# Layer 0's expert stage: a third bank for the up products, and gate, product, down product, result copy and store one to two steps later

## The chip, the cores and the metric

The kernel runs on one core of a Trainium2 chip. The metric is the device time of one execution in microseconds (us). It is given as the median of several runs; the profile comes from one further execution of the same program. The core's engines work side by side, each through its own list of instructions in order, and wait for each other by semaphores: TensorE (PE in the profile, its loads of weights PEld), VectorE (DVE), ScalarE (ACT), GpSimd (POOL) and SyncE (SP), which only issues transfers.

## The reference, cut to what matters

The program computes two layers. Each is a cross attention of 32 sequences of 128 tokens, width 128, over 77 context rows, and then a mixture of 8 experts of which every token uses 2. The change is in layer 0's experts:

```python
scores = x @ Wr.T + br                                  # 4096 tokens, 8 experts
idx    = top_k(scores + biases_N, 2)                    # two experts per token
val    = softmax(scores) at idx, divided by their sum
h      = x @ Wl1[n] + bl1[n]                            # 128 -> 512, a and b halves of 256
y      = (silu(a) * b) @ Wl2[n] + bl2[n]                # 256 -> 128
out    = sum over the token's two experts of val * y
x      = x + tanh(g_ffn[0]) * out
```

Layer 1 has attention with 16 heads and experts with one up product of 256, gelu and no biases.

## The kernel before, in words

**Blocks.** Tokens are sorted by expert. Each token's normalized row is scattered twice (once for each of its experts) into a list `x_rows` in device memory, and this list is worked through in blocks of 128 rows that share an expert: 71 blocks (0 to 70) in layer 0, 63 in layer 1. The block's result goes to `y_list`, also in device memory. Later GpSimd gathers for each of the 32 tiles of 128 tokens the two results of every token (`load`, two indirect transfers, line 1979), and VectorE adds them to the residual `x_res` (`combine`, line 1819).

**The plan.** `order()` (line 364) writes one list of tasks for the whole program. Every engine walks through the same list and issues its own part of each task, so the list fixes the order on every engine. `expert_steps` (line 302) yields the expert stage step by step. Before the change, step s of layer 0 had these tasks in this order:

1. `up` of block s-2. TensorE: four products of 128x128 into one bank of PSUM (line 1185), `UP_BANK[i % 2]`, two banks in turn. ScalarE, in the same task: the `gate`, silu of the first two quarters with bias, two instructions (line 1396).
2. `fetch` of a block some ten steps ahead. SyncE: one transfer from `x_rows` (line 869).
3. `turn` of block s. TensorE transposes the rows (line 1174); ScalarE copies them to `xb` (line 1379) and copies half of the expert's weights to a ring of four (line 1386); VectorE copies the other half (line 1783), after it has read the expert's number from a table.
4. `hide` of block s-2. VectorE: (third and fourth quarter + bias) * gate, two instructions (line 1791), written to `hidden`.
5. `down` of block s-4. TensorE: two products (line 1205) into `Y_BANK[i % 2]`. VectorE, in the same task: result plus bias to `y_sb` (line 1807).
6. `store` of block s-5. ScalarE's queue: one transfer of `y_sb` to `y_list` (line 1405).

Behind these a step can have late tasks: routing of the last tokens (steps 5 to 13: the tasks mturn, route, pick, rank and totals), the tables of the second part (blocks, steps 16 to 20, and block_bias at 22), at every second step from 30 to 44 one of eight `places` tasks (five VectorE instructions, lines 1750 to 1758), the loads and combines of tiles 0 to 11 (steps 53 to 73), and preparation of layer 1's attention (`clear`, `k1`, `k_load`, `norm`, `normalize`, `xt`, `q1`, `q_load`).

**Waits that matter here.** The up product of block i waits for `hidden` of block i-2, since both use one bank (line 1182). The down product of block i waits for the result copy of block i-2, for the same reason (line 1192). The gate of block i waits for `hidden` of block i-2 (the gate has two buffers). `hidden` has three buffers, `block_w` and `xb` four, `y_sb` six. The load of tile b waits for the stores of all blocks that can hold its tokens: for tiles 0 to 11 blocks 0 to 46. A tile's `gathered` buffer is one of three.

**Around the stage.** The first steps of the expert stage lie between the last steps of attention 0 (one each), and its last steps between the first of attention 1. Before the change steps 0 to 3 followed attention's steps 32 to 35; attention's step 35 has, among others, the normalization of the last group of tokens (line 1310, four ScalarE instructions, which wait until an earlier scatter has left the buffer) and a tanh (line 1373). At the other end 73 steps stood alone, and the first step of attention 1 (`score1`, line 1007, and VectorE's `row_max`, line 1445) followed step 73.

**Banks of PSUM.** There are eight. In the expert stage 0 and 1 are UP_BANK, 2 and 3 X_BANK (turns), 4 and 6 Y_BANK; SPLIT_BANK (5) and ROUTE_BANK (7) are used by the late tasks.

Of the kernel before, what the change touches and what calls it, by code (L numbers as in the profile page):

```python
# [66 lines left out]
UP_BANK = (0, 1)  # L67
X_BANK = (3, 2)
# [233 lines left out]
def expert_steps(layer, tasks, begun, after):  # L302
# [13 lines left out]
    for b in range(AMONG[layer]):  # L316
        begins = FIRST_DONE[layer] + 6 + (8 * b // 5 if layer == 0 else 11 * b // 10)
        loads.setdefault(begins, []).append(("load", layer, b))
        combines.setdefault(begins + 3, []).append(("combine", layer, b))
# [3 lines left out]
    for s in range(max(max(combines) + 1, n_blocks + 4 + (layer == 0))):  # L323
        step = []
        if 0 <= s - 2 < n_blocks:
            step.append(("up", first + s - 2))
        for _ in range(2):
# [6 lines left out]
        if layer == 0 and 0 <= s - 2 < n_blocks:  # L334
            step.append(("hide", s - 2))
        if 0 <= s - 4 < n_blocks:
            step.append(("down", first + s - 4))
        if 0 <= s - 4 - (layer == 0) < n_blocks:
            step.append(("store", first + s - 4 - (layer == 0)))
# [24 lines left out]
def order():  # L364
# [9 lines left out]
    phases = [(attention0_steps(tasks[0]), NSEQ), (expert_steps(0, tasks[0], NSEQ + 4, after0), BLOCKS[0] + 2),  # L374
# [21 lines left out]
def flamingo_two_layers(nc, a, out):  # L396
# [79 lines left out]
    with ExitStack() as stack:  # L476
# [261 lines left out]

        def hiddens(n):
# [184 lines left out]
        def _(pe):  # L924
# [7 lines left out]
            def split_task(t):  # L932
# [41 lines left out]
                else:  # L974
                    c0 = t[1] * GK
                    w.wait_ge("weights1", 6)
                    done = three_pass(banks[:, bank, 0:GK], w1_h[:, 1, :], w1_l[:, 1, :],
# [82 lines left out]
            for t in plan:  # L1060
# [114 lines left out]
                elif kind == "up":  # L1175
# [6 lines left out]
                    w.wait_ge("hidden", hiddens(i - 1))  # L1182
                    w.wait_ge("xb", i + 1)
                    for part in range(4 if layer == 0 else 2):
                        done = pe.matmul(banks[:, UP_BANK[i % 2], part * P:(part + 1) * P], block_w[:, i % WR, part // 2, part % 2 * P:(part % 2 + 1) * P], xb[:, i % BR, :],  # L1185
# [57 lines left out]
        def _(act):  # L1243
# [12 lines left out]
            for t in plan:  # L1256
# [131 lines left out]
                elif kind == "up":  # L1388
                    i = t[1]
                    layer, k, n = of_block(i)  # L1390
                    w.wait_ge("up", i + 1)
                    if layer == 0:
                        w.wait_ge("hidden", hiddens(i - 1))
                        w.wait_ge("block_bias", k + 1)
                        for half in (0, 1):
                            act.activation(gate[:, i % 2, half, :], banks[:, UP_BANK[i % 2], half * P:(half + 1) * P], ACT.Silu,  # L1396
                                           bias=block_bias[:, k, half, n:n + 1]).then_inc(sem("gate"))
                    else:
# [616 lines left out]
```

## Time and profile before

| | |
|---|---|
| runs | 740.4, 739.4, 742.06 us |
| median | 740.4 us |
| the profiled execution | 740.05 us |
| its span, first to last instruction | 738.3 us |
| mean granted clock of TensorE in it | 0.958 |
| busy: PE, PEld, DVE, ACT, POOL | 85%, 77%, 75%, 60%, 60% |
| layer 0's expert stage in the span | about 240 to 376 us |

How to read it: the times of the profile count from the span's start. "Busy" is the time in which an engine worked on an instruction. An idle time is put down to what ended it, the releaser; "issue" is time in which the engine waited for nothing that the profile shows. PE and PEld overlap. A line number is one of the kernel before.

### The profile page before, as it was taken

The numbers are of one execution on the slowest core, as the hardware profiler recorded it, in microseconds if no ns is written. First come the engines' busy times: TensorE is split into PE (matmuls) and PEld (weight loads), VectorE is DVE, ScalarE is ACT, GpSimd is POOL, SyncE is SP. The second block draws the span as 40 slices with busy tenths as digits, with TensorE's granted clock in tenths as the row PEclk, the third lists the DMA queues.
The fourth block names the chain that finished last, engine by engine and source line by source line (L and its number), as shares of the span: only waits on it lengthen the run. The fifth ranks groups of instructions, "written<-read, shape, count | busy, mean of one in ns | idle before, by whom it ended". The sixth has DMA issues, their size and how long they took to land.

```text
span 738.3 us, 16455 instructions
## 1 busy us (share of the span) xinstructions
PE 624.7 (85%) x4501; PEld 566.0 (77%) x4501; DVE 555.6 (75%) x1931; ACT 443.0 (60%) x1275; POOL 442.1 (60%) x658
## 2 busy tenths in 40 slices
PE   6879789888885889789877888889979898789997
PEld 5668778888775779789766777778868787579885
DVE  3368588888886588888778879868897795655784
ACT  2477567867754556567666666756766654434462
POOL 4034347778766642305658778876756668766752
PEclk9999999999997999999989999989999999999999
DMA  9445658444432345335524525424234102423455
GB/s 259 138 118 135 183 169 221 130 134 137 139 112 78 99 125 157 89 95 143 155 72 121 122 73 111 123 58 120 90 79 108 44 21 89 129 89 96 146 173 165
DMA packets 132774, 89.48 MB, mean 121 GB/s; under 512 B 31508, under 2 KB 121780, under 8 KB 132652
## 3 DMA queue, kind: packets, MB, share of 16 engines
q1 hardware_dynamic: 108540, 62.83, 32.1%
q0 software_dynamic: 7904, 17.19, 7.3%
q10 hardware_dynamic: 16240, 8.41, 4.0%
q8 instruction: 38, 0.62, 0.4%
q14 instruction: 52, 0.43, 0.2%
HBM read 50.73 MB, written 39.85 MB: 123 GB/s over the span
## 4 chain that ended last, share of the span: by engine, by line
PE 37%; DVE 27%; ACT 14%; issue 8%; POOL 7%; DMA 3%; SPq 2%; DVEq 2%; ACTq 0%; POOLq 0%
PE banks L1185 7%; PE banks L1048 5%; PE banks L1205 4%; POOL gathered L1979 3%; ACT prob L1317 2%; DVE row_max L1445 2%; PE banks L1226 2%; PE banks L928 2%; PE banks L1033 2%; PE banks L1216 2%; PE banks L1015 2%; DVE row_max L1492 1%; ACT xm L1310 1%; ACT vo L1327 1%; POOL v_flat L1932 1%
## 5 line engine op out<-in xcount | busy, mean ns | idle before, releaser
L1970 POOL DMA_INDIRECT x_rows<-xm,row x120 | 121.0, 1008 | 36.2 <-issue 27.9
L1185 PE MATMUL banks<-xb,up 128*128 128x128 f32 x820 | 119.9, 284 | 24.4 <-DVE hidden L1791 11.6
L1185 PEld LDWEIGHTS banks<-xb,up 128*128 128x128 f32 x820 | 106.3, 197 | 35.4 <-issue 13.9
L1979 POOL DMA_INDIRECT gathered<-y_list,row x64 | 62.6, 978 | 52.4 <-issue 51.1
L1048 PE MATMUL banks<-v_flat,prob_t 128*128 128x108 f32 (+2 forms) x640 | 85.6, 282 | 8.4 <-POOL v_flat L1932 6.0
L1048 PEld LDWEIGHTS banks<-v_flat,prob_t 128*128 128x128 f32 (+1 forms) x640 | 78.5, 195 | 17.1 <-issue 10.6
L1342 ACT ACTIVATE prob_t<-banks 128x512 f32<-128x512 f32 x192 | 73.4, 440 | 26.8 <-PE banks L1015 25.9
L1205 PE MATMUL banks<-down,hidden 128*128 x536 | 83.6, 280 | 1.7 <-DVE y_sb L1809 1.2
L1985 POOL DMA_INDIRECT y_rows<-y_sb,result_at x63 | 60.7, 964 | 30.5 <-issue 12.1
L1932 POOL TENSOR_TENSOR v_flat<-v_raw,row_head 104x64 f32<-104x64 f32 (+1 forms) x128 | 55.8, 464 | 32.1 <-ACT v_raw L1358 31.7
L1205 PEld LDWEIGHTS banks<-down,hidden 128*128 128x128 f32 x536 | 72.2, 196 | 2.3 <-issue 2.3
L1898 POOL TENSOR_TENSOR prob<-prob,inv_sum 128x616 f32<-128x616 f32 x32 | 39.1, 1223 | 54.7 <-DVE inv_sum L1508 54.6
L1396 ACT ACTIVATE gate<-banks,block_bias 128x128 f32<-128x128 f32 x142 | 44.2, 363 | 41.2 <-PE banks L1185 39.4
L1445 DVE TENSOR_REDUCE row_max<-banks 128x8 f32<-128x616 f32 x64 | 50.3, 786 | 9.1 <-PE banks L1007 9.1
L1015 PE MATMUL banks<-ident,prob 128*128 128x128 f32 (+1 forms) x375 | 55.8, 281 | 0.3 <-POOL prob L1898 0.3
L1783 DVE COPY up<-up 128x256 f32 x134 | 42.9, 320 | 16.4 <-issue 8.3
L1033 PE MATMUL banks<-vo_flat,prob_t 128*128 128x128 f32 (+1 forms) x320 | 48.7, 307 | 5.1 <-ACT prob_t L1342 2.9
L1033 PEld LDWEIGHTS banks<-vo_flat,prob_t 128*128 128x128 f32 (+1 forms) x320 | 45.6, 219 | 6.3 <-ACT prob_t L1342 3.9
L1791 DVE SCALAR_TENSOR_TENSOR hidden<-banks,block_bias,gate 128x128 f32<-128x128 f32 x142 | 42.8, 343 | 9.0 <-ACT gate L1396 8.0
L1317 ACT ACTIVATE prob<-banks,row_max 128x77 f32<-128x77 f32 x128 | 30.8, 324 | 29.7 <-DVE row_max L1492 29.7
L1015 PEld LDWEIGHTS banks<-ident,prob 128*128 128x128 f32 (+1 forms) x375 | 45.6, 146 | 1.5 <-POOL prob L1898 0.5
L1358 ACT ACTIVATE v_raw<-banks 128x512 f32<-128x512 f32 x64 | 28.0, 437 | 30.8 <-PE banks L1107 30.8
(251 smaller groups left out, 1660.4 us busy)
## 6 DMA issues: line engine op xcount, KB each, us to landing
vo_flat<-v_rows SPq DMA_DIRECT2D x32, 256.0 KB
x_norm<-x_rows SPq DMA_DIRECT2D x74, 72.0 KB
v_rows<-vo SPq DMA_DIRECT2D x38, 128.0 KB
y_list<-y_sb ACTq DMA_DIRECT2D x71, 64.0 KB
x_far<-x_rows SPq DMA_DIRECT2D x60, 72.0 KB
q_rows<-up_raw SPq DMA_DIRECT2D x8, 512.0 KB
q_even<-q_rows SPq DMA_DIRECT2D x12, 256.0 KB
q_odd<-q_rows SPq DMA_DIRECT2D x12, 256.0 KB
```

What stands on the lines that cost most here:

```text
L1015: done = pe.transpose(banks[0:chunk_rows[c], PT_BANK[k], c % 4 * SEQ:(c % 4 + 1) * SEQ], flat[:, c * P:c * P + chunk_rows[c]], ident[:, :])
L1033: done = pe.matmul(banks[:, O_BANK, 0:D], prob_t[0:rows, b % 2, c, :], vo_flat[0:rows, b % 2, c, :], start=c == 0, stop=c == CHUNKS - 1)
L1048: done = pe.matmul(banks[:, O_BANK, half * width:half * width + cols], prob_t[0:rows, u % 2, c, :], v1_flat[0:rows, first:first + cols], s ...
L1185: done = pe.matmul(banks[:, UP_BANK[i % 2], part * P:(part + 1) * P], block_w[:, i % WR, part // 2, part % 2 * P:(part % 2 + 1) * P], xb[: ...
L1205: done = pe.matmul(banks[:, Y_BANK[i % 2], 0:D], hidden[:, i % HR, half, :], of_expert(flat[:, (2 * layer + half) * D:], i, D), start=half ...
L1317: done = act.activation(prob[:, b % 2, h, :], banks[:, S_BANK[1], h % 4 * NKEY:(h % 4 + 1) * NKEY], ACT.Exp, bias=row_min[:, b % 2, h:h + ...
L1342: act.activation(dst, banks[0:rows, PT_BANK[k], 0:len(chunks) * SEQ], ACT.Copy).then_inc(sem("prob_t"))
L1445: dve.tensor_reduce(m_view, s_view, AX.X, ALU.max).then_inc(sem("row_max"))
L1932: pool.tensor_tensor(v1_rows[0:rows, b % 2, half, chunks[0]:chunks[-1] + 1, :, 0:DK1], v1_raw[0:rows, chunks[0]:chunks[-1] + 1, half, :, : ...
L1970: pool.indirect_dma_start(out=x_rows[layer][:, :], out_offset=bass.IndirectOffsetOnAxis(ap=row[:, n, c:c + 1], axis=0), in_=xm[:, i % 2, j ...
L1979: pool.indirect_dma_start(out=gathered[:, b % GR, n, :], out_offset=None, in_=y_list[0:blocks_of_tile(0, b) * P, :], in_offset=bass.Indire ...
L1985: pool.indirect_dma_start(out=y_rows[:, :], out_offset=bass.IndirectOffsetOnAxis(ap=result_at[:, i % (2 * YR):i % (2 * YR) + 1], axis=0), ...
```

## The change

Layer 0's up products get three banks in turn: 0, 1 and a third, which is SPLIT_BANK for blocks below 28 and ROUTE_BANK from there on. The wait for `hidden` becomes that of the block which had the bank before. Up products in SPLIT_BANK wait for the last split of attention 0, those in ROUTE_BANK for the last biases, and `k1` waits until the first 28 blocks are hidden.

In layer 0 the parts of a block are tasks of their own and come later. In step s: `up` s-2 as before, `gate` s-3 (was s-2), `turn` s as before, `hide` s-3 (was s-2), `down` s-5 (was s-4), `keep`, the result copy, s-6 (was s-4, with down), `store` s-7 (was s-5). Loads and combines of layer 0 begin two steps later, and with them the preparation of attention 1; 75 steps stand alone instead of 73. In layer 1 down, keep and store stand in one step as before.

```diff
+UP_SWITCH = 28
@@ expert_steps
-        begins = FIRST_DONE[layer] + 6 + (8 * b // 5 if layer == 0 else 11 * b // 10)
+        begins = FIRST_DONE[layer] + (8 + 8 * b // 5 if layer == 0 else 6 + 11 * b // 10)
...
-    for s in range(max(max(combines) + 1, n_blocks + 4 + (layer == 0))):
+    for s in range(max(max(combines) + 1, n_blocks + (7 if layer == 0 else 4))):
...
             step.append(("up", first + s - 2))
+        if layer == 0 and 0 <= s - 3 < n_blocks:
+            step.append(("gate", s - 3))
...
-        if layer == 0 and 0 <= s - 2 < n_blocks:
-            step.append(("hide", s - 2))
-        if 0 <= s - 4 < n_blocks:
-            step.append(("down", first + s - 4))
-        if 0 <= s - 4 - (layer == 0) < n_blocks:
-            step.append(("store", first + s - 4 - (layer == 0)))
+        if layer == 0:
+            if 0 <= s - 3 < n_blocks:
+                step.append(("hide", s - 3))
+            if 0 <= s - 5 < n_blocks:
+                step.append(("down", s - 5))
+            if 0 <= s - 6 < n_blocks:
+                step.append(("keep", s - 6))
+            if 0 <= s - 7 < n_blocks:
+                step.append(("store", s - 7))
+        elif 0 <= s - 4 < n_blocks:
+            step += [("down", first + s - 4), ("keep", first + s - 4), ("store", first + s - 4)]
@@ order
-    phases = [(attention0_steps(tasks[0]), NSEQ), (expert_steps(0, tasks[0], NSEQ + 4, after0), BLOCKS[0] + 2),
+    phases = [(attention0_steps(tasks[0]), NSEQ), (expert_steps(0, tasks[0], NSEQ + 4, after0), BLOCKS[0] + 4),
@@ new functions
+        def up_bank(i):
+            if i >= BLOCKS[0]:
+                return UP_BANK[i % 2]
+            return (UP_BANK[0], UP_BANK[1], SPLIT_BANK if i < UP_SWITCH else ROUTE_BANK)[i % 3]
+        def up_before(i):
+            first = 0 if i < BLOCKS[0] else BLOCKS[0]
+            return max([j for j in range(first, i) if up_bank(j) == up_bank(i)], default=first - 1)
@@ TensorE, k1
+                    w.wait_ge("hidden", 2 * UP_SWITCH)
@@ TensorE, up
-                    w.wait_ge("hidden", hiddens(i - 1))
+                    w.wait_ge("hidden", hiddens(up_before(i) + 1))
+                    if up_bank(i) == SPLIT_BANK:
+                        w.wait_ge("split_lo", xt_count(NG - 1))
+                    elif up_bank(i) == ROUTE_BANK:
+                        w.wait_ge("block_bias", 2)
@@ ScalarE (waits and instructions of the gate as before, in a task of their own)
-                elif kind == "up":
+                elif kind == "gate":
...
+                elif kind == "up" and t[1] >= BLOCKS[0]:
@@ VectorE
-                elif kind == "down":
+                elif kind == "keep":
```

## Rows read from the trace of the kernel before

**Rows 1.** Stretches: busy us (instructions) PE, PEld, DVE, ACT, POOL; clock, DMA share, GB/s.

```profile
296.00:330.00 34.00, 27.08 (x226) 25.67 (x225) 29.27 (x110) 18.99 (x68) 6.67 (x6) 1.00 0.35 92
...
330.00:345.00 15.00, 15.00 (x137) 15.00 (x137) 11.93 (x43) 11.54 (x43) 5.01 (x6) 1.00 0.51 136
```

**Rows 2.** Timeline of one free step: start, duration, instruction, idle before.

```profile
340.08 1.06 PE L1185 MATMUL banks<-xb,up 128*128 128x128 f32 x8
...
340.98 0.27 PE L1174 MATMUL banks<-ident,x_norm 128*128 128x128 f32 x1
...
341.08 0.61 PE L1205 MATMUL banks<-down,hidden 128*128 x4
...
341.18 0.62 ACT L1396 ACTIVATE gate<-banks,block_bias 128x128 f32<-128x128 f32 x2 [0.35 <-PE banks L1185]
...
341.53 1.06 PE L1185 MATMUL banks<-xb,up 128*128 128x128 f32 x8
...
341.69 0.28 ACT L1379 ACTIVATE xb<-banks 128x128 f32<-128x128 f32 x1
...
341.83 0.61 DVE L1791 SCALAR_TENSOR_TENSOR hidden<-banks,block_bias,gate 128x128 f32<-128x128 f32 x2
...
342.38 0.29 DVE L1807 TENSOR_TENSOR y_sb<-banks,down_bias 128x128 f32<-128x128 f32 x1
```

**Rows 3.** Groups by line, 240 to 376 us: busy, mean ns, idle before.

```profile
L1185 PE MATMUL banks<-xb,up 128*128 128x128 f32 x568 | 78.6, 283 | 17.0 <-DVE hidden L1791 11.6 <-ACT up L1386 2.2 <-DVE up L1783 2.0
...
L1205 PE MATMUL banks<-down,hidden 128*128 x284 | 44.3, 280 | 0.4 <-DVE y_sb L1807 0.4
```

**Rows 4.** Timeline, the start of the expert stage.

```profile
238.62 1.28 ACT L1396 ACT_TABLE_LOAD   x1
...
241.65 0.62 ACT L1396 ACTIVATE gate<-banks,block_bias 128x128 f32<-128x128 f32 x2 [1.74 <-PE banks L1185]
...
244.13 1.13 PE L1185 MATMUL banks<-xb,up 128*128 128x128 f32 x8 [1.41 <-DVE hidden L1791]
...
244.71 1.65 ACT L1310 ACTIVATE xm<-x_res,m_shift,m_rstd 128x128 f32<-128x128 f32 x4 [1.96 <-DMA x_rows<-xm,row]
...
246.35 0.60 ACT L1396 ACTIVATE gate<-banks,block_bias 128x128 f32<-128x128 f32 x2
...
246.99 0.61 DVE L1791 SCALAR_TENSOR_TENSOR hidden<-banks,block_bias,gate 128x128 f32<-128x128 f32 x2 [1.90 <-ACT gate L1396]
...
247.31 0.61 ACT L1396 ACTIVATE gate<-banks,block_bias 128x128 f32<-128x128 f32 x2
...
247.85 1.13 PE L1185 MATMUL banks<-xb,up 128*128 128x128 f32 x8 [2.03 <-DVE up L1783]
```

**Rows 5.** Timeline, weight copies of VectorE one places period apart.

```profile
316.64 0.29 DVE L1783 COPY up<-up 128x256 f32 x1
...
320.58 0.29 DVE L1783 COPY up<-up 128x256 f32 x1
```

**Rows 6.** Timeline of ScalarE, the table load of attention 1.

```profile
376.71 1.28 ACT L1332 ACT_TABLE_LOAD   x1
...
378.02 0.72 ACT L1332 ACTIVATE prob<-prob 128x616 f32<-128x616 f32 x1
```

**Rows 7.** The chain that ended last, at the first gathers: start, duration.

```profile
335.93 1.53 DMA y_list<-y_sb
...
338.47 1.05 POOL gathered L1979
...
347.32 4.05 DMA gathered<-y_list,row
```

**Rows 8.** Timeline: last gather, last combine, attention 1 first row_max.

```profile
371.90 0.94 POOL L1979 DMA_INDIRECT gathered<-y_list,row  x1 [0.30 <-issue]
...
375.71 0.73 DVE L1819 SCALAR_TENSOR_TENSOR x_res<-gathered,token_w,x_res 128x128 f32<-128x128 f32 x2
...
376.36 0.79 DVE L1445 TENSOR_REDUCE row_max<-banks 128x8 f32<-128x616 f32 x1
```

More of the change, by code:

```diff
@@ L1181, in _ @@
                     w.wait_ge("shifted", NSEQ + layer * U1)
-                    w.wait_ge("hidden", hiddens(i - 1))
+                    w.wait_ge("hidden", hiddens(up_before(i) + 1))
[3 more added lines that the diff above has]
+                        w.wait_ge("block_bias", 2)
                     w.wait_ge("xb", i + 1)
                     for part in range(4 if layer == 0 else 2):
-                        done = pe.matmul(banks[:, UP_BANK[i % 2], part * P:(part + 1) * P], block_w[:, i % WR, part // 2, part % 2 * P:(part % 2 + 1) * P], xb[:, i % BR, :],
+                        done = pe.matmul(banks[:, up_bank(i), part * P:(part + 1) * P], block_w[:, i % WR, part // 2, part % 2 * P:(part % 2 + 1) * P], xb[:, i % BR, :],
                                          start=True, stop=True)
@@ L1387, in _ @@
                                        ACT.Copy).then_inc(sem("block_w_act"))
-                elif kind == "up":
+                elif kind == "gate":
                     i = t[1]
-                    layer, k, n = of_block(i)
+                    _, k, n = of_block(i)
                     w.wait_ge("up", i + 1)
[L1392 to L1398, printed above, removed]
-                        w.wait_ge("y_mm", i - HR + 1)
-                        act.activation(hidden[:, i % HR, :, :].rearrange("p t n -> p (t n)"), banks[:, UP_BANK[i % 2], 0:HID1], ACT.Gelu).then_inc(sem("hidden"))
+                    w.wait_ge("hidden", hiddens(i - 1))
+                    w.wait_ge("block_bias", k + 1)
+                    for half in (0, 1):
+                        act.activation(gate[:, i % 2, half, :], banks[:, up_bank(i), half * P:(half + 1) * P], ACT.Silu,
+                                       bias=block_bias[:, k, half, n:n + 1]).then_inc(sem("gate"))
+                elif kind == "up" and t[1] >= BLOCKS[0]:
+                    i = t[1]
+                    w.wait_ge("up", i + 1)
+                    w.wait_ge("y_mm", i - HR + 1)
+                    act.activation(hidden[:, i % HR, :, :].rearrange("p t n -> p (t n)"), banks[:, up_bank(i), 0:HID1], ACT.Gelu).then_inc(sem("hidden"))
                 elif kind == "store" and t[1] < BLOCKS[0]:
@@ L1790, in _ @@
                     for half in (0, 1):
-                        dve.scalar_tensor_tensor(hidden[:, i % HR, half, :], banks[:, UP_BANK[i % 2], (2 + half) * P:(3 + half) * P],
+                        dve.scalar_tensor_tensor(hidden[:, i % HR, half, :], banks[:, up_bank(i), (2 + half) * P:(3 + half) * P],
                                                  block_bias[:, k, 2 + half, n:n + 1], gate[:, i % 2, half, :], ALU.add, ALU.mult).then_inc(sem("hidden"))
-                elif kind == "down":
+                elif kind == "keep":
                     i = t[1]
```

## The prediction

> **What bounds the kernel now.** I read clock and span first (one core, nothing disturbed), then busy time by stretches, the idle time ahead of the up products, and last the timeline of the expert stage and of what follows it. The change touches layer 0's expert stage alone, roughly 240 to 376 us of the 738.3 us span.
>
> Where the stage runs freely TensorE is full: busy 15.00 of 15.00 us [rows 1], and one step follows the other in 1.45 us (up products at 340.08 and 341.53) [rows 2]. A step is 13 passes (8 up, 1 turn, 4 down) of about 0.11 us. There the 0.35 us that ScalarE waits ahead of each gate costs nothing, and a third bank gives nothing: the next up product already starts without a wait.
>
> What can be won is TensorE's idle time ahead of the up products, 17.0 us in all, against 0.4 us ahead of the down products [rows 3]. Going through the timeline I sort the 18 waits of over 0.2 us into three kinds:
> - The start: two waits, 1.41 and 2.03 us. VectorE's hidden product waited 1.90 us for a gate, and ScalarE had stood 1.96 us before it on the scatter of x_rows [rows 4].
> - Eight waits on the two-step beat of "places" between 300 and 330 us, 6.9 us in sum. There TensorE is busy 27.08 of 34 us, VectorE 29.27 [rows 1]. VectorE has two steps' and one places' work from the weight copy at 316.64 to the one at 320.58, nearly without a gap: 3.94 us [rows 5]. TensorE needs 2.90. VectorE is the bound.
> - Eight single waits, 6.5 us in sum, each behind a long VectorE task (totals, tables, norm).
>
> **The change part by part.**
>
> *Banks and lag.* Call U the end of a step's up product (341.14). Now the gate starts right after U, hidden ends at U+1.30 and the result copy at U+1.53 [rows 2]. The up product two steps on reuses the bank and starts at U + 2 x 1.45 - 1.06 = U+1.84, so VectorE may be 0.54 us late. After the change the gate stands behind xb and weight copy of the step before. That xb can start with the end of the turn, about U+0.16 (340.98 + 0.27, and a signal). Gate, xb and copy take ScalarE 0.96 us when it catches up (246.35, 247.31 [rows 4]), 0.51 of them from gate to xb, so 0.45 from xb to the next gate: U+0.61. Gate 0.62, then hidden until U+1.9 and the copy until U+2.1. With three banks hidden has until U+3.29. But the result copy has its own date: down of block s-5 still waits for the copy of s-7, and this is now issued one step before it, where it was two. That down starts as an up product ends (341.08), so at U+2.84. The slack is 0.7 us instead of 0.54: the third bank is undone by the two banks of Y_BANK. I expect 0.18 us from each single wait, 8 x 0.18 = 1.4, and 0.18 once from the places stretch, where VectorE's work stays what it is and only its lead at the beginning counts: 1.6. Against it, VectorE reads route, rank and totals in the same step in which TensorE makes them; there it has no lead, while its date is earlier by one step (1.45, less the 0.85 us by which its step otherwise ends earlier: 0.6). I charge that once. Taken: **-1.0 us**. Ends: -6.8 (8 waits x 0.85, if all the lead came through) and +3.0 (five such steps at 0.6).
>
> *The table load at the start.* ACT_TABLE_LOAD for the gate's function stands right ahead of the first gate: 1.28 us at 238.62, and ScalarE had nothing to do until 241.65 [rows 4]. That of attention's exp likewise stands right ahead of its first exp [rows 6]. Gate 0 moves from step 2 to step 3, and between them lie attention's last tasks, the four normalizations that wait for the scatter until 244.71 among them. So the load would start at about 246.35, where gate 1 now starts, on the path that runs from the normalizations through gate and hidden (246.99) to the up product at 247.85 [rows 4]. Gate 0 takes gate 1's place, and the fourth up product still needs the xb and the weight copy behind it. The cover was ScalarE's idle time; without it nothing hides the load: **+1.28 us**. Other end: 0, if it is placed earlier.
>
> By the Trainium skill, "ScalarE: Activation LUTs", section "What ACT_TABLE_LOAD costs", a switch is the load's 1283 ns and a drain of about 1380 ns. The trace has the first figure and not the second: the next activation starts at 378.02, 0.03 us behind the load's end [rows 6]. By the page the sum below would be 1.4 us higher.
>
> *Stores and gathers.* GpSimd's gathers of layer 0's results are a chain of their own: 24 of them at 1.25 us (0.95 and 0.30 of issue), 2.5 us for a tile, while tiles come up every 8/5 steps, 2.32 us. So the steps don't pace GpSimd once it has started. It starts at 338.47, behind the store of block 46, which the chain has from 335.93; its eighth gather took 4.05 us to land [rows 7]. Its last starts at 371.90, the last combine at 375.71 (3.81 us on) and attention's first row_max right behind, at 376.36 [rows 8]. The change puts store, load and combine two steps later: +2.90. The store stands behind xb, which no longer waits for the gate pair (0.51 us [rows 2]): -0.5. That the drain's steps are short doesn't help, for it is GpSimd that is late. At the far end there is some slack: of the 34.4 us from 338.47 to 372.84 the gathers take 24 x 1.25 = 30.0, and not all of the rest (norm, waits for combines) need recur. Taken -0.5. Sum **+1.9 us**. Ends: +2.9, and +0.5 if there is slack enough to leave the drain alone.
>
> *Drain.* One down product (0.61) and one result copy (0.28) more now stand ahead of attention's first score, partly beside gate and hidden of the last block: +0.5. The gathers' +1.9 lies beside it and hides it.
>
> *The rest.* Store and copy of one y_sb slot stay five steps apart; hidden and block_w keep their distances. k1's new wait for 56 hidden halves is passed when k1 comes (step 34, block 27 hidden at step 30). ROUTE_BANK is used from block 29 on, after the biases of step 22. Fetches, queues and tails on SP are as far ahead of their turns as before. Layer 1 gets the same instructions in the same order. All 0, with these distances as cover. Attention 1 hangs on its first row_max, and GpSimd on VectorE there, so I pass the shift on whole; 0 is the other bound, if a later wait swallows it.
>
> Sum: +1.28 - 1.0 + 1.9 = **+2.2 us**. The profiled execution took 740.05 us (span 738.3 and 1.75 around it) and becomes 742.2. The median of the three runs is 740.4, 0.35 above it: **742.6 us**.
>
> **The rivals.**
> 1. *The lead comes through, and the kernel gets faster.* If the copy's date doesn't bind, each single wait shrinks by up to 0.85, and the start's 1.41 us (block 2 no longer waits for block 0's bank) may stay won: -6.8 + 1.9 + 1.28 - 1.41 = -5.0; with half the lead -1.6. For it: 11.6 of the 17.0 us are waits for hidden, exactly what the third bank loosens [rows 3]. Against: the VectorE-bound stretch, and Y_BANK. It decides from about 0.5 us a wait. Time 735.4 to 738.8; I take 738.
> 2. *Only one of the two costs is real* (the load is placed earlier, or the gathers have slack): between +0.3 and +1.3, 741.2. For it: the last gather's slack can't be read, and the load's place is my inference from two rows.
> 3. *The early date of the copy binds often:* +3.0 in place of -1.0, 746.6. For it: five steps read TensorE in the same step. Against: in most long waits VectorE is late by its own work [rows 5].
> 4. *A switch costs more than its load*, the engine being drained beside it. The 0.03 us behind the load would then be over 1 us; with 1.4 it gives 744.0. The rows speak against it [rows 6]. It is the page's rule named above.
>
> **How the numbers follow.** Forecast 0.46, rival 1 0.22, rival 2 0.22, rival 3 0.06, rival 4 0.04. About 0.3% (2.2 us) can be told from no change here. The forecast lies on that bound: its own range is 741.3 to 744.5, 0.28 of its 0.46 above 742.6. Slower: 0.28 + 0.06 + 0.04 and 0.02 of rival 2, 0.40. Within: 0.18 + 0.20 + 0.03 of rival 1 at its least, 0.41. Faster: 0.19. The range that holds 8 in 10 goes from 737.6, about rival 1's value, to 745.4.
>
> **What would show it.** The table load between normalizations and first gate, and the fourth up product some 1.3 us later. Idle time of several us ahead of the down products (0.4 now), released by the y_sb copy, and less ahead of the up products with hidden nearly gone as releaser, the sum of both within 2 us of 17.4. Steps of 1.45 us and, on places, 3.9 for two. The first gather 2 to 3 us after 338.47, and the first row_max at 378 to 379. The prediction is wrong if the idle sum falls by over 4 us, if the load is where it was, or if the last combine isn't held up by a gather.

## The result and the profile after

The changed kernel took 751.7 us in the median of four runs (748.1 to 753.1), the kernel before 740.6 in four: ratio 1.0126, 95% interval 1.0100 to 1.0152. The forecast was 742.6, its range 737.6 to 745.4; the kernel got slower by 11 us. The profiled execution of the changed kernel is its fastest: 748.09 us, span 746.4, 8.1 us over the span before. So the trace accounts for 8.1 of the 11 us; the rest lies between executions. Lines below: L1209 is the up product, L1229 the down product, L1419 the gate, L1403 xb, L1410 ScalarE's weight copy, L1430 the store, L1816 hidden, L1832 the result copy, L1470 row_max.

Where the 8.1 us arise is read from the timelines, by the start of xb for a block of the stage, then the first row_max of attention 1 and the span. Two of the experiments stand beside it:

| | block 2 | 6 | 30 | 48 | 62 | 70 | row_max | span |
|---|---|---|---|---|---|---|---|---|
| before, start in us | 242.16 | 253.05 | 295.29 | 331.55 | 352.61 | 370.63 | 376.36 | 738.3 |
| changed | +1.6 | +3.6 | +6.2 | +5.5 | +7.2 | +7.1 | +8.5 | +8.1 |
| third bank alone | +1.1 | -1.1 | -2.4 | -3.4 | -3.9 | -3.1 | -2.9 | -1.9 |
| changed, copy with its down product | +1.7 | +3.0 | +1.7 | +2.1 | +2.5 | +2.2 | +4.3 | +6.2 |

The first 1.1 to 1.7 us, up to block 2, come before the changed work and differ from execution to execution. After that the changed kernel loses 2.0 us in four blocks (2 to 6), 2.6 until block 30, gives back 0.8 beside "places" (blocks 30 to 48), loses 1.7 where the kernel before ran free (48 to 62), and 1.4 from the last block to row_max.

The groups by line, 240 to 385 us (busy, mean ns, idle before and its releasers), against [rows 3]:

```profile
L1209 PE MATMUL banks<-xb,up 128*128 128x128 f32 x568 | 80.9, 287 | 5.4 <-DVE hidden L1816 4.4 <-ACT up L1410 0.6
...
L1229 PE MATMUL banks<-down,hidden 128*128 x284 | 46.3, 286 | 10.3 <-DVE y_sb L1832 10.2
...
L1419 ACT ACTIVATE gate<-banks,block_bias 128x128 f32<-128x128 f32 x142 | 44.4, 365 | 7.0 <-DVE y_sb L1832 2.6 <-PE banks L1209 0.9 <-issue 0.7
...
L1403 ACT ACTIVATE xb<-banks 128x128 f32<-128x128 f32 x69 | 19.2, 278 | 22.0 <-PE banks L1194 20.4 <-issue 1.0
```

The waits of the up products for hidden have become waits of the down products for the copy: the idle time was 17.0 us ahead of the up products and 0.4 ahead of the down products, and is 5.4 and 10.3 now. The sum, 15.7 against 17.4, is even lower. The loss hides in the busy time: up products 80.9 us against 78.6, down products 46.3 against 44.3. Part of it is passes at half clock at the start of the stage (below). The larger part isn't. From block 6 to block 30, before and after (busy us of PE, PEld, DVE, ACT, POOL, granted clock, DMA share, GB/s):

```profile
253.05:295.29 42.24, 38.61 (x335) 37.65 (x333) 34.93 (x149) 26.49 (x100) 15.21 (x25) 1.00 0.50 137
```

```profile
256.69:301.52 44.83, 41.49 (x336) 38.44 (x335) 34.85 (x150) 30.97 (x99) 14.09 (x22) 1.00 0.43 120
```

The clock is 1.00 in both, the passes are the same number, and the listed waits are no longer (3.1 us of down products, 3.6 us of up products before). Yet the passes take 2.9 us more. The records of neighbouring passes overlap (one is 0.27 us long and the next starts 0.10 us behind it, [rows 2]), so a short delay between two of them counts as busy. The loss is in longer steps: of the steps of 1.45 us, the best pace, the kernel before has seven in this stretch, the changed one two; most of its others take 1.52 us and more. Nor are the long waits what costs: eight of the 14 waits of the down product, 4.8 of their 10.2 us, stand beside "places", where the kernel before waited 6.9 us and the changed one gives time back.

The start of the stage, answering to [rows 4] (start, duration, instruction, idle before):

```profile
246.31 1.65 ACT L1334 ACTIVATE xm<-x_res,m_shift,m_rstd 128x128 f32<-128x128 f32 x4 [1.77 <-DMA x_rows<-xm,row]
247.86 0.19 ACT L1397 ACTIVATE lead_t<-lead 128x4 f32<-128x4 f32 x1
248.07 1.28 ACT L1419 ACT_TABLE_LOAD   x1
249.36 0.63 ACT L1419 ACTIVATE gate<-banks,block_bias 128x128 f32<-128x128 f32 x2
...
250.96 2.05 PE L1209 MATMUL banks<-xb,up 128*128 128x128 f32 x8 [4.06 <-DVE hidden L1816]
...
253.01 1.06 PE L1229 MATMUL banks<-down,hidden 128*128 x4
```

The table load stands between normalizations and first gate, as forecast. Behind it stands an idle time of 4.06 us, and what follows it is slow: the eight passes of the up product take 2.05 us, the four of the down product 1.06 (1.06 to 1.13 and 0.61 in [rows 2, 4]). The windows show the clock (columns as above):

```profile
246.00:250.00 4.00, 0.90 (x8) 0.66 (x6) 0.45 (x3) 3.66 (x9) 3.02 (x4) 0.93 0.25 74
250.00:254.00 4.00, 3.04 (x14) 3.07 (x15) 2.58 (x9) 2.60 (x10) 3.08 (x4) 0.50 0.16 55
254.00:258.00 4.00, 4.00 (x28) 4.00 (x27) 1.10 (x4) 2.37 (x8) 2.24 (x4) 0.71 0.22 75
```

TensorE was busy 0.90 of 4 us, and the granted clock of the next 4 us is 0.50, the lower of its two levels (1.2 GHz). This isn't wholly new. The kernel before has such passes too, behind its own wait of 2.03 us [rows 4]; its up product there:

```profile
250.63 1.87 PE L1185 MATMUL banks<-xb,up 128*128 128x128 f32 x8
```

It has 16 passes at half clock there (4 of a down product at 248.93, 4 of another task, these 8), the changed kernel 24. Eight more at 0.11 us are, by estimate, 0.9 us.

And two steps of the stretch that ran free before, answering to [rows 2]:

```profile
343.94 1.06 PE L1209 MATMUL banks<-xb,up 128*128 128x128 f32 x8
...
344.55 0.63 ACT L1419 ACTIVATE gate<-banks,block_bias 128x128 f32<-128x128 f32 x2
...
345.14 0.28 ACT L1403 ACTIVATE xb<-banks 128x128 f32<-128x128 f32 x1
...
345.48 1.13 PE L1209 MATMUL banks<-xb,up 128*128 128x128 f32 x8
345.53 0.42 ACT L1410 ACTIVATE up<-up 128x256 f32 x1
345.56 0.33 ACTq L1430 DMA_DIRECT2D y_list<-y_sb  x1
...
345.99 0.62 ACT L1419 ACTIVATE gate<-banks,block_bias 128x128 f32<-128x128 f32 x2
...
346.72 0.61 DVE L1816 SCALAR_TENSOR_TENSOR hidden<-banks,block_bias,gate 128x128 f32<-128x128 f32 x2 [0.16 <-ACT gate L1419]
...
347.25 0.28 DVE L1832 TENSOR_TENSOR y_sb<-banks,down_bias 128x128 f32<-128x128 f32 x1
...
347.92 0.63 ACT L1419 ACTIVATE gate<-banks,block_bias 128x128 f32<-128x128 f32 x2 [0.35 <-DVE y_sb L1832]
```

Steps take 1.54 us here (343.94, 345.48, 347.02) instead of 1.45. ScalarE has no gap: from gate to gate it takes 1.44 us, 0.59 to xb and 0.85 from xb to the next gate. The weight copy starts 0.39 us behind xb. Between them the program has the read of the expert's number into a register. In the kernel before, where ScalarE had 0.35 us to spare, the same copy starts 0.16 us behind xb (341.69 in [rows 2]) and is done 0.59 us behind xb's start:

```profile
341.85 0.43 ACT L1386 ACTIVATE up<-up 128x256 f32 x1
342.62 0.62 ACT L1396 ACTIVATE gate<-banks,block_bias 128x128 f32<-128x128 f32 x2 [0.35 <-PE banks L1185]
```

So the same instructions filled 1.10 of 1.45 us before and fill 1.44 when they stand gate to gate without a gap. At 347.92 the gate even waits for the copy: by the program, the store ahead of it in ScalarE's queue waits for it.

The gathers, answering to [rows 7, 8]:

```profile
349.01 1.06 POOL L2004 DMA_INDIRECT gathered<-y_list,row  x1 [40.89 <-DMA y_list<-y_sb]
...
381.37 1.04 POOL L2004 DMA_INDIRECT gathered<-y_list,row  x1 [0.30 <-issue]
...
384.18 0.73 DVE L1844 SCALAR_TENSOR_TENSOR x_res<-gathered,token_w,x_res 128x128 f32<-128x128 f32 x2
384.82 0.79 DVE L1470 TENSOR_REDUCE row_max<-banks 128x8 f32<-128x616 f32 x1
```

The first gather comes 10.5 us later than before, the last 9.5, the last combine 8.5. What the end hangs on has changed too. In the chain that ended last, the kernel before has no gather behind 351.4 us: it goes on through TensorE and the copy of the last result. The changed kernel's runs through nine gathers in a row and the transfer of a tenth, to a combine that waits 0.41 us for its data. From the two chains, before and after (start, duration):

```profile
375.51 0.29 DVE y_sb L1807
```

```profile
376.00 5.22 DMA gathered<-y_list,row
...
383.97 0.29 DVE y_sb L1832
```

But in both kernels it is the last result copy that stands right ahead of the last combine (375.51 and 375.71, 383.97 and 384.18). So the drain is on this path, beside the gathers.

### The profile page after: what moved, and what is told of

It is laid out like the page before. It is cut to its first block, busy times and chain, and to the rows that moved or that the text cites. A ratio compares the mean times of both kernels' runs of the same rounds, so it can differ in the third digit from the quotient of the medians.

```text
span 746.4 us, 16462 instructions
## 1 busy us (share of the span) xinstructions
PE 634.7 (85%) x4501; PEld 571.0 (77%) x4501; DVE 554.3 (74%) x1931; ACT 455.8 (61%) x1275; POOL 442.8 (59%) x658
## 4 chain that ended last, share of the span: by engine, by line
PE 35%; DVE 23%; ACT 11%; issue 9%; POOL 7%; SPq 6%; DMA 6%; DVEq 2%; ACTq 0%; POOLq 0%
PE banks L1209 7%; PE banks L1068 5%; PE banks L1229 5%; SPq L864 4%; POOL gathered L2004 3%; DMA v_rows<-vo 2%; DVE row_max L1470 2%; ACT prob L1341 2%; PE banks L947 2%; PE banks L1035 2%; PE banks L1127 2%; PE banks L1250 1%; ACT vo L1351 1%; POOL x_rows L1995 1%; POOL v_flat L1957 1%
## 5 line engine op out<-in xcount | busy, mean ns | idle before, releaser
L1209 PE MATMUL banks<-xb,up 128*128 128x128 f32 x820 | 121.8, 287 | 13.2 <-DVE up L1808 6.2
L1209 PEld LDWEIGHTS banks<-xb,up 128*128 128x128 f32 x820 | 107.6, 199 | 25.2 <-DVE up L1808 10.6
L1229 PE MATMUL banks<-down,hidden 128*128 x536 | 86.1, 285 | 11.1 <-DVE y_sb L1832 10.2
L1229 PEld LDWEIGHTS banks<-down,hidden 128*128 128x128 f32 x536 | 72.0, 195 | 16.5 <-issue 15.8
L1470 DVE TENSOR_REDUCE row_max<-banks 128x8 f32<-128x616 f32 x64 | 50.4, 788 | 8.4 <-PE banks L1027 8.4
L1816 DVE SCALAR_TENSOR_TENSOR hidden<-banks,block_bias,gate 128x128 f32<-128x128 f32 x142 | 42.9, 344 | 16.4 <-ACT gate L1419 13.9
L1403 ACT ACTIVATE xb<-banks 128x128 f32<-128x128 f32 x134 | 37.0, 276 | 26.9 <-PE banks L1194 25.3
L1419 ACT ACTIVATE gate<-banks,block_bias 128x128 f32<-128x128 f32 x142 | 44.4, 365 | 7.0 <-DVE y_sb L1832 2.6
```

The source lines that it names most:

```text
L1209: done = pe.matmul(banks[:, up_bank(i), part * P:(part + 1) * P], block_w[:, i % WR, part // 2, part % 2 * P:(part % 2 + 1) * P], xb[:, i ...
L1229: done = pe.matmul(banks[:, Y_BANK[i % 2], 0:D], hidden[:, i % HR, half, :], of_expert(flat[:, (2 * layer + half) * D:], i, D), start=half ...
L1470: dve.tensor_reduce(m_view, s_view, AX.X, ALU.max).then_inc(sem("row_max"))
```

## The experiments

The chips are not alike: the kernel before takes 742 us on chip 7 and 789 to 794 on chips 2, 9, 13 and 15. So each ratio is to the kernel before on the same chip. The changed kernel itself gave 1.0126, 1.0090 (chip 13) and 1.0047 (chip 9), so a gap of under 0.008 between kernels on different chips says little. A name in brackets is the kernel's in the tables and texts below.

Theory at the start: the copy's early date, with only two result banks, costs the down products their slack. Rivals: ScalarE's full queue, the table load, the late output.

**Chip 2: one part alone, one part undone.** Third bank alone (third_bank):

```diff
-  up(s-2), gate(s-3) | turn(s), hide(s-3), down(s-5), keep(s-6), store(s-7)
+  up(s-2), gate(s-2) | turn(s), hide(s-2), down(s-4), keep(s-4), store(s-5)
   three up banks; loads and combines from step 6, two phases overlapping as before
```

> The kernel before with the third bank for up products alone; gate, product, down product, copy and stores stand in their old steps. Base 740.6 us. Theory A (the new order costs, the bank alone gives): the up product no longer waits for the hidden rows of the block before, so most of the 17.0 us of [rows 3] is gone; if the order of steps is all that stands against it, 733 to 738 us. Theory B (the bank gives nothing, since the next engine in the step is as late): 740 to 742 us, with the idle time of the up product turned into idle time before the down product. Theory C (the waits for the two other tenants of banks 5 and 7 cost): over 742 us.

0.9953 (0.9925 to 0.9981): faster than the kernel before. Theory A, with a gain at its lower end (0.0047 of 790 us are 3.7 us).

Late output alone (late_out: two banks; stores, gathers, combines and the next phase two steps later):

```diff
-  store(s-5); loads from FIRST_DONE + 6; alone = BLOCKS[0] + 2
+  store(s-7); loads from FIRST_DONE + 8; alone = BLOCKS[0] + 4
```

> The kernel before, two banks, old steps for gate, product, down product and copy; only stores two steps later, gathers and combines two steps later, and the two phases overlap two steps less. Theory A (the gather chain sets the end, so each step of delay reaches it): plus 2.9 us for two steps of 1.45 us, 743.5 us, with row_max of attention 1 later by 2 to 3 us. Theory B (the middle, as predicted): plus 1.9 us, 742.5. Theory C (nothing, the delay hides): 740.6.

1.0001 (0.9970 to 1.0032). The bounds are 2.5 us either way, so it tells nothing against the 1.9 us of the sum. Its trace says more. From the last block's xb to the first row_max it takes 6.9 us, the third bank alone on the same chip 6.1, the kernel before on chip 13 6.3: two steps of late output cost 0.6 to 0.7 us there, and no combine waits for a gather.

Copy in its down product's step (copy_with_down):

```diff
-  down(s-5), keep(s-6)
+  down(s-5), keep(s-5)
```

> The changed kernel with the result copy in the step of its down product instead of one later; all else as changed (751.4 us, ratio 1.0126). Theory A (the early date of the copy, two result banks, is what binds): the waits of the down product for the copy, 10.2 us in sum, go, and the time falls by 4 us or more, to 747 or less. Theory B (ScalarE's queue sets the step and makes gates late): the down product instead waits for the product of ScalarE's late gate; the time stays at 750 to 752.

0.9981 (0.9958 to 1.0003). Theory A, and more than it said: all of the loss is gone on this chip.

The first gate's table load pulled ahead (early_table):

```diff
+  elif kind == "up" and t[1] == 0:
+      act.activation(early_act, gates[:, 0:1], ACT.Silu)
```

> The changed kernel with one Silu of one element on ScalarE ahead of the first gate, where the gate stood before, so that the table load comes back into the idle time after the last exponential. Theory A: the first gate comes 1.3 us earlier (the load) and the fourth up product is not at half clock, 1 us more; 749.0 to 750.0 us. Theory B (the start's delay is made up later in the stage): no change, 751.4 us.

1.0070 (1.0038 to 1.0102), near the changed kernel's. Against copy_with_down, on the same chip, the intervals don't meet: the date of the copy is worth 0.009, 7 us, even with the table load out of the way. The load's own part shows in the traces: with the Silu blocks 2 to 6 take 13.0 us on the slower chips (this kernel and early_table_down below), without it, with the gate late, 13.9 to 14.1, and 13.8 in the kernel before.

**Chip 13: both kernels again, and the late copy without the late gate.**

> The changed kernel, unchanged, on the chip on which the others ran (before: 790.2 us there). Ratio 1.0126 on the first chip; if the loss is the order's and not the chip's: ratio 1.006 to 1.014, 795 to 801 us, and one Silu ahead of it (795.1 us, 1.007) saved 0 to 2 us.

1.0090 (1.0057 to 1.0123). The 790.2 us of the expectation are chip 2's; the kernel before takes 792.4 here.

> The kernel before, for its trace on this chip: about 790 us, the 50 us over the first chip in waits for transfers and in the granted clock, spread over all stages; its stage of layer 0's experts about as long as on the first chip.

792.4 us; span 790.6 against 738.3, granted clock 0.931 against 0.958. The stage was not as long as on the first chip: block 2 to the first row_max took 160 us against 134, and ScalarE waited there for an unknown queue (in total, times, longest), which the first chip's trace doesn't have:

```profile
ACT gate L1396 <- remote: 22.8, 4, 6.9
```

Third bank with the copy, and output, one step later (late_copy):

```diff
-  down(s-4), keep(s-4), store(s-5)
+  down(s-4), keep(s-5), store(s-6)
```

> Third bank with gate, product and down product in their old steps, and the result copy alone one step later (stores, gathers one step later with it). Base: third bank alone, 0.9953 (786.4 us at 790.2 before). Theory A (the copy's date binds, two result banks): the down product waits for the copy as in the changed kernel, some 10 us in sum, and 4 to 8 us reach the end: 790 to 794 us, ratio 1.000 to 1.005. Theory B (the copy's date costs only where the gate is late too, since ScalarE has no slack): 786 to 788 us, ratio 0.995 to 0.998.

1.0158 (1.0091 to 1.0225): theory A, at two to four times its price (the third bank alone ran on chip 2, but the gap of 0.02 is larger than any shift between chips). TensorE's waits, 245 to 415 us (in total, times, longest), in the third bank alone and here:

```profile
PE banks L1229 <- DVE y_sb L1832: 2.5, 2, 2.1
```

```profile
PE banks L1229 <- DVE y_sb L1832: 29.4, 23, 5.5
```

Third bank alone with its stores on SyncE's queue (third_bank_sp):

```diff
-  scalar:  act.dma_start(y_list[...], y_sb[...])
+  sync:    sync.dma_start(y_list[...], y_sb[...])
```

> Third bank alone, with layer 0's stores issued from SyncE's queue instead of ScalarE's. Theory A (ScalarE's order, 0.33 us for each store, limits the step): 71 stores by 0.33 us are 23 us of ScalarE; a tenth to a quarter of it reaches the end, 2 to 6 us less than the third bank alone: 780 to 784 us. Theory B (ScalarE has slack): 786 to 787 us. Theory C (SyncE waits for the copy and its row loads come late): 788 us or more.

1.0142 (1.0081 to 1.0204), theory C in sign. VectorE's waits show another place than it named: the copy waits for its slot's old store to land.

```profile
DVE y_sb L1832 <- DMA y_list<-y_sb: 12.3, 9, 2.4
```

So ScalarE's store issue is not what to take away, at least not to that queue.

**Chip 15: where the copy stands.** In the changed kernel, the copy ahead of hidden on VectorE (copy_first):

```diff
-  hide(s-3), down(s-5), keep(s-6)
+  keep(s-6), hide(s-3), down(s-5)
```

> The changed kernel with the result copy ahead of the product (gate times up) in each step's order on VectorE; all dates else as changed (ratio 1.009 on this chip). Theory A (the copy is late because it stands behind a product that waits for a gate just begun; the down product two blocks on waits for the copy): the idle time before the down product falls from 11 us in 250:370 to under 4, ratio 0.995 to 1.000. Theory B (ScalarE's late gates set the step, wherever the copy stands): ratio 1.007 to 1.010.

1.0041 (1.0012 to 1.0070), between the two. The changed kernel wasn't run on chip 15 (1.0047 to 1.0126 elsewhere), so it isn't shown that this order gains anything. The wait did not fall, it is longer than the changed kernel's 12.7 and 14.1 us on chips 13 and 9; theory A's "under 4" is wrong:

```profile
PE banks L1229 <- DVE y_sb L1832: 17.6, 17, 3.7
```

Gate and hidden back in the up product's step, all later parts as changed (gate_old_place):

```diff
-  gate(s-3), hide(s-3)
+  gate(s-2), hide(s-2)
```

> The changed kernel with gate and product back in the step of their up product; down product, copy, store one to two steps later as changed. Theory A: the copy of block s-7, on which the down product of step s waits, then stands behind the product of block s-3, whose up product is of the same step, instead of that of s-4: the same order as in the third bank with a late copy alone (1.0158), so worse than the changed kernel: 1.012 to 1.018. Theory B (the late gate on ScalarE is what costs): better than the changed kernel, 0.998 to 1.005.

1.0273 (1.0206 to 1.0340): in theory A's direction, beyond its range, and against B, by which an earlier gate should help.

```profile
PE banks L1229 <- DVE y_sb L1832: 29.5, 21, 7.3
```

But the edit did a second thing, which neither theory has. `hidden` has three buffers, and the product of block i waits for the down product of block i-3. With the product in step i+2 and the down product in step i+5, that down product stands in the same step as the product that waits for it. VectorE's waits (in total, times, longest), none of this kind in the third bank alone:

```profile
DVE hidden L1816 <- PE banks L1229: 16.9, 28, 1.7
```

So 1.0273 is not the price of the copy's place alone; how it divides isn't shown.

On late_copy, the copy ahead of hidden (late_copy_first):

```diff
-  hide(s-2), down(s-4), keep(s-5)
+  keep(s-5), hide(s-2), down(s-4)
```

> Third bank, gate, product and down product in old steps, copy one step later but ahead of the product in VectorE's order (behind it: 1.0158). Theory A (the place behind the product is what made the date early): 0.993 to 1.000, the idle time before the down product from 19.5 us to under 4. Theory B (the step later itself costs, for want of a third result bank): 1.010 or more.

1.0080 (1.0040 to 1.0121): between the theories, above the third bank's 0.9953 and below late_copy's 1.0158, whose interval it touches, on another chip. The wait for the copy is 17.6 us against 29.4. Both the place behind hidden and the step seem to count; the shares aren't shown.

And copy_with_down with the Silu of early_table added (early_table_down):

```diff
-  keep(s-6)
+  keep(s-5); act.activation(early_act, gates[:, 0:1], ACT.Silu) ahead of gate 0
```

> The changed kernel with the copy in the down product's step (0.9981) and one Silu ahead of the first gate. Theory A (the exposed table load costs 1.3 to 2 us to the end): 0.9955 to 0.9965. Theory B (made up later): 0.998.

1.0054 (1.0023 to 1.0085), above both theories; copy_with_down has no time on this chip, so both were compared on chip 7.

**Chip 7, on which the kernel before takes 742 us: the rest of the loss.**

The first three repeat kernels above, unchanged; a 2 behind the name marks the repeat. The changed kernel itself has no time on this chip.

> Third bank alone, again, in one call with the next three. If it is surely faster than the kernel before: ratio 0.993 to 0.997. If the first result was a drift between calls: 0.998 to 1.002.

0.9969 (0.9943 to 0.9995), 738.4 us against 741.8: surely faster, twice.

> The changed kernel with the copy in its down product's step, again. If the terms of the prediction hold beside the copy's date (table load 1.3, output two steps later 1.9 us): 0.003 to 0.005 above third_bank_2, 0.997 to 1.001. If gate and output cost nothing: equal to third_bank_2.

1.0062 (1.0035 to 1.0088), 0.009 above the third bank; on chip 2 it was 0.003.

> copy_with_down with one Silu ahead of the first gate. If the exposed table load reaches the end: 0.0016 to 0.0025 below copy_with_down_2. If it is made up later: equal within 0.0015. Above it by more than 0.003 would say that the Silu itself does harm, as the single call before seemed to (1.0054).

1.0050 (1.0022 to 1.0078): equal within what a run can tell; the Silu does no harm. In its trace blocks 2 to 6 take 10.2 us, without it 12.2, and 13.3 in out_earlier; but block 2 came 2.8 us later than without it.

Copy_with_down with its output one step earlier (out_earlier):

```diff
-  store(s-7); loads from FIRST_DONE + 8; alone = BLOCKS[0] + 4
+  store(s-6); loads from FIRST_DONE + 7; alone = BLOCKS[0] + 3
```

> copy_with_down with stores, gathers, combines and the second layer's start one step earlier (one step later than in the kernel before instead of two). If each step of late output reaches the end in half to whole (0.95 to 1.45 us): 0.0012 to 0.0018 below copy_with_down_2. If the gathers are not what sets the start of the next layer: equal.

1.0066 (1.0041 to 1.0090): equal by medians. From the last block's xb to row_max the traces lose against before: third bank alone (output not moved) 0.2 us, output one step later 1.1, two steps later 2.1 and 2.7, and 1.4 in the changed kernel. In these the gate and the down product are later as well, so more of the last blocks' work lies behind that xb; late_out, with late output alone, lost only 0.6 to 0.7.

These traces also show what the copy's date does where the kernel before ran free. In copy_with_down_2 ScalarE's order is the changed kernel's, and steps are back at 1.45 us (12 of the 13 that the trace shows whole in blocks 48 to 62; in the changed kernel 2 of 9, the others 1.52 to 1.82):

```profile
338.71 1.06 PE L1209 MATMUL banks<-xb,up 128*128 128x128 f32 x8
340.16 1.06 PE L1209 MATMUL banks<-xb,up 128*128 128x128 f32 x8
341.61 1.06 PE L1209 MATMUL banks<-xb,up 128*128 128x128 f32 x8
```

So ScalarE's full queue doesn't set the step by itself. Nor does the store that follows its copy by one step, as in the changed kernel: so it does in out_earlier, and the steps are 1.45 there too (339.05, 340.50, 341.95).

What does TensorE wait for? Its waits in third_bank_2 (240 to 376 us):

```profile
PE banks L1209 <- ACT up L1410: 6.8, 8, 1.4
...
PE banks L1209 <- DVE up L1808: 1.5, 1, 1.5
```

and in copy_with_down_2, with gate, hidden, down and copy one step later together (240 to 382 us):

```profile
PE banks L1209 <- DVE hidden L1816: 16.2, 13, 4.6
...
PE banks L1229 <- DVE y_sb L1832: 1.6, 1, 1.6
```

With the gate in its old step, three banks end every wait for hidden. With the gate a step later the up products wait 16.2 us for it, 4.6 of them at the start, as they did with two banks (11.6). The late gate spends the step that the third bank gave. From block 6 to 70 that costs 1.2 us (116.8 against 115.6).

**Chip 9: gate and hidden, or the down product?** (down_later)

```diff
   out_earlier, and
-  gate(s-3), hide(s-3)
+  gate(s-2), hide(s-2)
```

> Third bank, gate and product (gate times up) in their old step, down product, copy, store, gathers one step later. Differs from out_earlier (1.0066) in gate and product alone. If the gate and product a step later are what costs beside the copy's date (they spend the step of slack that the third bank gives the up product, and leave the pipeline a step longer at its start): as third bank alone, 0.995 to 0.999. If the down product's step is what costs: 1.004 to 1.007.

0.9994 (0.9975 to 1.0013), between the theories. It has the same side effect as gate_old_place, `hidden`'s three buffers with product and down product three steps apart:

```profile
DVE hidden L1816 <- PE banks L1229: 9.7, 6, 3.2
```

So it doesn't tell the down product's step from a shortage of `hidden` buffers either.

> The changed kernel on this chip: 1.009 to 1.013 whichever theory holds, 0.004 to 0.007 of it the copy's date.

1.0047 (1.0021 to 1.0072), below expectation. It is above down_later on the same chip, and the intervals don't meet. In down_later TensorE waits for no hidden, as in the third bank alone, and little for the copy:

```profile
PE banks L1229 <- DVE y_sb L1832: 3.6, 2, 2.2
```

Ordered by that one wait (245 to 415 us of the traces, the four slower chips):

| kernel | down waits for copy, us | ratio |
|---|---|---|
| third bank alone | 2.5 | 0.9953 |
| late_out | 3.2 | 1.0001 |
| down_later | 3.6 | 0.9994 |
| copy_with_down | 4.1 | 0.9981 |
| early_table_down | 4.2 | 1.0054 |
| third_bank_sp | 9.3 | 1.0142 |
| changed, chip 13 | 12.7 | 1.0090 |
| changed, chip 9 | 14.1 | 1.0047 |
| early_table | 17.6 | 1.0070 |
| copy_first | 17.6 | 1.0041 |
| late_copy_first | 17.6 | 1.0080 |
| late_copy | 29.4 | 1.0158 |
| gate_old_place | 29.5 | 1.0273 |

All six kernels whose copy stands a step behind its down product are slower than before, at 12.7 us of such waits or more. Of the six with both in one step four are at 1.0001 or below; early_table_down at 1.0054 isn't explained by this wait, and third_bank_sp has its stores to pay for. On chip 7 the wait orders nothing: the three kernels with the late gate have 1.0 to 2.2 us of it and stand at 1.0050 to 1.0066. And the changed kernel has more of it on the chip where it lost less. So the wait is a sign of the copy's date, not its price.

## Why the prediction was wrong

**The step that failed: the slack of the copy.** The mechanism was named ("the third bank is undone by the two banks of Y_BANK"), its size was not. The prediction let 0.45 us pass from xb to the next gate, read from 246.35 and 247.31 [rows 4], where ScalarE caught up and issued no store. In a running step of the changed kernel it is 0.85. Put into the prediction's own sum: the gate starts not at U+0.61 but U+0.99 (U 345.00, gate 345.99), the copy ends not at U+2.1 but U+2.53 (347.53), and the date U+2.84 leaves 0.31 us where 0.7 was counted and 0.54 had been. So each late task of VectorE costs 0.23 us more rather than 0.18 less. And a delay that the prediction charged once recurs: the down product waits for the copy 14 times, 10.2 us. The term of -1.0 measured +3.5 (block 6 to block 70, +3.6 to +7.1): 2.6 in blocks 6 to 30 and 1.7 in blocks 48 to 62, mostly as longer steps and not as listed waits, and 0.8 back beside "places". With the copy in the down product's step the same stretch measures -0.8. The path from a late copy to the many short delays is not shown step by step; that they go with the copy's date is. This is rival 3's cause; it was given a chance of 0.06. Its price, +3.0, was near, but by luck: it was five steps of 0.6 us that read TensorE in the same step, and the loss lies elsewhere too. It was argued away with "in most long waits VectorE is late by its own work". VectorE's lateness was absorbed as long as the copy was due two steps on.

**ScalarE.** That its 0.35 us of waiting cost nothing was true and misled: without the gap the same work takes 1.44 us of a 1.45 us step. The late gate has ScalarE at that, and behind it the store waits for the copy and holds the next gate (2.6 us in 5 waits). By itself this doesn't lengthen the steps (copy_with_down_2, out_earlier); it makes the copy later.

**The table load** came where it was put and costs its 1.28 us there: 0.01 us separates its end (249.35) from the gate. By the Trainium skill, "ScalarE: Activation LUTs", "What ACT_TABLE_LOAD costs", a drain of about 1380 ns would come on top; this row doesn't show it either, and rival 4 falls. What was missed is the clock: the wait grew to 4.06 us, and eight more passes behind it ran at 1.2 GHz. Block 2 to block 6 lost 2.0 us instead of 1.28, near the 1.28 and the 0.9 estimated above. Whether that reaches the end stays open: the medians of the pair on chip 7 differ by 0.0012, inside their intervals.

**Stores and gathers**, +1.9, and **drain**, +0.5 and hidden: the two together measured 1.4 us in the changed kernel. The size is near, the split isn't shown. Late output alone cost 0.6 to 0.7 us in its trace; the last result copy stands right ahead of the last combine, so the drain wasn't hidden; and the reading that "it is GpSimd that is late" doesn't fit the end of the chain before, which has no gather behind 351.4 us. The first gather was forecast 2 to 3 us later and came 10.5 us later. **Places**: the stretch itself gave 0.8 us back, as VectorE-bound as read.

**Not foreseen:** that the third bank alone is worth 2.3 to 3.7 us. The prediction saw it undone by the result banks alone; what undoes it is also the gate's later step (16.2 us of waits for hidden come back, and 3.5 us between blocks 2 and 6 on chip 7). Rival 1 had this gain, for a kernel that didn't keep it.

**Open.** How the 0.009 between third bank alone and copy_with_down on chip 7 divides over gate, down product, table load and output: the traces give 3.5 us of it to blocks 2 to 6, 1.2 to the rest of the stage and 1.9 to the stretch from the last xb to row_max. The one run that would split gate from down product (down_later) was on chip 9, where copy_with_down has no time (0.9981 on chip 2), and it brought a wait of its own for `hidden`'s buffers. Why the same change costs 0.5 to 1.3% by chip is not settled; on the slower chips ScalarE also waits for an unknown queue. Whether such waits cover others isn't shown. A third result bank was not tried: all eight banks have tenants here.

**Best version:** the third bank alone, 0.9969 and 0.9953.

## What to carry to other kernels

When a stage is put later in a software pipeline, count the steps between each producer and its consumer for every buffer, not the buffers that grew: here the up bank gained a step and the result bank lost one. That holds for experiments too: two of those here moved the product and the down product three steps apart over three `hidden` buffers, and so measured two things. Don't take an engine's gap for reserve: ScalarE's 1.10 us of work with a gap of 0.35 became 1.44 us without the gap. Don't read the loss off the sum of waits: here it fell while the kernel got slower, since short delays count as busy; compare the busy time of equal work. And time the added buffer alone: it gave 0.3 to 0.5%, and the reordering turned this into a loss of 0.5 to 1.3%.

## What was not expected of the hardware

- The same kernel takes 741 us on the first chip and 742 on chip 7, and 789 to 794 on four others (granted clock 0.958 on the first chip, 0.931 on chip 13); the ratio of one change varied between chips, from 1.0047 to 1.0126.
- An up product straight behind 4.06 us of idle TensorE ran at 0.50 of the clock (8 passes 2.05 us against 1.13), and the clock was at 0.71 in the following 4 us.
- ScalarE's weight copy starts 0.16 us behind the start of xb where the engine has a gap in the step, and 0.39 us behind it where it has none.
- 71 stores moved from ScalarE's queue to SyncE's, which carries the row loads, went with 12.3 us in which the copies waited for old stores to land, and with 1.9% against the same kernel on another chip.
